# Expert rows added onto x by the gathering transfers, in the third attention

## The reference, cut to what matters

```
x = x + L1_ffn(layernorm(x))      # top 2 of 8 experts per token
x = x + L2_xattn(layernorm(x), ctx)

def L1_ffn(x):
    top_scores, token_idx, counts = route(x, gate_w, 8, 2)
    routed_in = x[token_idx] * top_scores[:, None]
    routed_out = grouped_swiglu(routed_in, w1, w2, w3, eid)
    return zeros.at[token_idx].add(routed_out)

def L2_xattn(x, context):         # 8 heads of 64, 64 keys per sequence
    q, k, v = x @ Wq, context @ Wk, context @ Wv
    return softmax(q k^T / 8) v @ Wo + bo
```

## Time and profile before

| | us |
|---|---|
| median of 3 runs (1964.0 to 1968.96) | 1968.83 |
| the profiled execution, its own time | 1969.98 |
| its span in the profile | 1967.4 |
| PE busy over the span | 1397.9 (71%) |
| DVE busy | 1165.4 (59%) |
| ACT busy | 714.6 (36%) |
| POOL busy | 590.0 (30%) |

### The profile page before, as it was taken

How to read it: one execution, slowest core, us unless ns; L and a number is a source line. 1 busy time by engine, 2 the same in 40 slices (tenths; PEclk the granted TensorE clock), 3 DMA queues, 4 the chain that set the end, 5 groups by cost and what they waited for, 6 DMA issues and landing times. The chain is left out here.

```text
span 1967.4 us, 43981 instructions
## 1 busy us (share of the span) xinstructions
PE 1397.9 (71%) x14780; PEld 1068.0 (54%) x14780; DVE 1165.4 (59%) x3326; ACT 714.6 (36%) x1769; POOL 590.0 (30%) x1118
## 2 busy tenths in 40 slices
PE   6999889965999730099948999740099646566564
PEld 3777645533777520099936888630088534454453
DVE  4888578877888760044424555460011179969896
ACT  2666456655666400022213455310033212232232
POOL 4555111112110116500047652117500187211231
PEclk9999956777999855599978999955599967677576
DMA  4222100000000001177731110001277511010001
GB/s 147 51 51 51 29 1 2 3 3 18 23 19 22 8 0 45 56 195 206 205 92 44 41 43 24 8 0 47 65 195 201 142 43 35 1 33 11 1 1 43
DMA packets 109071, 108.50 MB, mean 55 GB/s; under 512 B 12656, under 2 KB 88432, under 8 KB 108784
## 3 DMA queue, kind: packets, MB, share of 16 engines
q1 hardware_dynamic: 100720, 89.61, 16.7%
q0 software_dynamic: 8192, 16.79, 3.0%
HBM read 81.19 MB, written 25.17 MB: 54 GB/s over the span
## 5 line engine op out<-in xcount | busy, mean ns | idle before, releaser
L2223 DVE COPY e_xT<-e_pX 128x256 f32<-128x256 f32 x72 | 30.6, 425 | 317.2 <-PE e_pX L2284 317.2
L2284 PE MATMUL e_pX<-W,e_rows 128*128 128x128 f32 x144 | 28.7, 282 | 213.8 <-DMA e_rows<-slots_in 212.6
L2295 PE MATMUL e_H<-e_xT,e_w_up 128*128 128x256 f32 x736 | 174.9, 386 | 1.1 <-DMA e_w_up<-in_f_dram 1.1
L2295 PEld LDWEIGHTS e_H<-e_xT,e_w_up 128*128 128x128 f32 x736 | 136.9, 194 | 18.1 <-DVE e_xT L2223 1.5
L2284 PEld LDWEIGHTS e_pX<-W,e_rows 128*128 128x128 f32 x144 | 18.5, 147 | 216.4 <-DMA e_rows<-slots_in 216.0
L2305 PEld LDWEIGHTS e_pY<-e_w_down,e_h 128*128 128x128 f32 x992 | 119.6, 192 | 23.2 <-issue 16.6
L2305 PE MATMUL e_pY<-e_w_down,e_h 128*128 128x128 f32 x992 | 124.8, 277 | 10.2 <-ACT e_h L2272 9.0
L2144 POOL DMA_INDIRECT slots_in<-R,r_put x96 | 92.0, 959 | 57.1 <-issue 29.0
L428 DVE TENSOR_REDUCE a_mx<-a_S 128x8 f32<-128x1024 f32 x64 | 78.1, 1221 | 34.3 <-PE a_S L513 34.1
L473 ACT ACTIVATE a_PT<-a_ST 128x1024 f32<-128x1024 f32 x64 | 65.5, 1023 | 79.2 <-PE a_ST L540 79.2
L2261 ACT ACTIVATE e_silu<-e_H 128x256 f32<-128x256 f32 x120 | 46.0, 383 | 124.0 <-PE e_H L2295 124.0
(11 more groups left out here) (414 smaller groups left out, 4071.8 us busy)
## 6 DMA issues: line engine op xcount, KB each, us to landing
e_w_up<-in_f_dram SPq DMA_DIRECT2D x40, 384.0 KB, 3.7
e_w_down<-in_f_dram SPq DMA_DIRECT2D x32, 322.0 KB, 3.1
e_rows<-slots_in SPq DMA_DIRECT2D x72, 128.0 KB, 3.0
slots_out<-e_y SPq DMA_DIRECT2D x72, 128.0 KB, 3.6
e_w_up<-in_f_dram SPq DMA_DIRECT2D x32, 256.0 KB, 3.7
e_w_down<-in_f_dram SPq DMA_DIRECT2D x40, 192.0 KB, 3.3
slots_in<-Y SPq DMA_DIRECT2D x32, 160.0 KB, 2.5
a_cK<-in_ctxT_dram SPq DMA_DIRECT2D x64, 64.0 KB, 1.9
```

Source lines behind the costliest of these rows:

```text
L2295: i = nc.tensor.matmul(H[:, banks * p + b, CHUNK * c:CHUNK * (c + 1)], up[:, p, at:at + P], xT[:, p, :], start=True, stop=True)
```

## The change

POOL no longer adds rows. The two gathers of a tile write onto X itself, with an addition in the transfer; the second is issued only when the first has landed (`gather_onto_x`, k = 1). DVE waits for both of them itself (`rows_added`, in front of the statistics), and the statistics no longer wait for `s_x`. POOL's lags become 7 for the bias (8 before), 4 for `pool_rstd` (5 before), 0 for the first gather and 2 for the second. The order on POOL is bias, rstd, first gather, second gather. In this stage Y and R are no longer used. The whole diff:

```
--- before.py
+++ after.py
@@ -1108,7 +1108,7 @@
         s_pt, s_pts, s_o, s_rd, s_zn = [sem(n) for n in ("pt", "pt_out", "o", "rden", "zn")]
         s_zt, s_zts, s_y, s_x = [sem(n) for n in ("zt", "zt_out", "y", "x")]
         combine = Combine(net, net.routing, sem)
-        ln = LayerNorm(net, sb, sem, xn, s_xt, combine.s_x)
+        ln = LayerNorm(net, sb, sem, xn, s_xt, None)
         block = ctx.enter_context(nc.Block())
 
         @block.sync
@@ -1135,12 +1135,15 @@
                 done(pool, ln.s_xn, u)
                 nc.gpsimd.tensor_tensor(X[:, u, :], X[:, u, :], w("a2_bo"), ALU.add).then_inc(s_bo, 1)
 
-            pipeline(pool, NT, [(IN_FLIGHT + 4, add_bias), (IN_FLIGHT, lambda u, p: combine.add(pool, u)),
-                                (IN_FLIGHT + 1, lambda u, p: ln.pool_rstd(pool, u, p)),
-                                (0, lambda u, p: combine.gather(u))], straight=True)
+            pipeline(pool, NT, [(7, add_bias), (4, lambda u, p: ln.pool_rstd(pool, u, p)),
+                                (0, lambda u, p: combine.gather_onto_x(pool, u, 0)),
+                                (2, lambda u, p: combine.gather_onto_x(pool, u, 1))], straight=True)
 
         @block.vector
         def _(dve):
+            def rows_added(u, p):
+                combine.arrive(dve, u)
+
             def take_k(u, p):
                 done(dve, s_k, u)
                 free(dve, s_S, u)
@@ -1173,7 +1176,7 @@
                 nc.vector.tensor_tensor(X[:, u, :], pV[:, 0:128], X[:, u, :], ALU.add).then_inc(s_x, 1)
 
             pipeline(dve, NT, [(10, normalise), (7, softmax), (5, take_k),
-                               (0, lambda u, p: ln.vector_stats(dve, u, p)),
+                               (0, rows_added), (0, lambda u, p: ln.vector_stats(dve, u, p)),
                                (1, lambda u, p: ln.vector_moments(dve, u, p)),
                                (2, lambda u, p: ln.vector_apply(dve, u, p)), (11, residual)], straight=True)
 
@@ -2353,13 +2356,15 @@
         done(dve, self.s_first, u)
         v.tensor_tensor(pair(net.X, u), pair(net.X, u), rows[1], ALU.add).then_inc(self.s_x, 1)
 
-    def add(self, pool, u):
-        net = self.net
-        self.arrive(pool, u)
-        x, rows = net.X[:, u, :], (net.Y[:, u, :], net.R[:, u, :])
-        net.nc.gpsimd.tensor_tensor(x, x, rows[0], ALU.add).then_inc(self.s_first, 1)
-        done(pool, self.s_first, u)
-        net.nc.gpsimd.tensor_tensor(x, x, rows[1], ALU.add).then_inc(self.s_x, 1)
+    def gather_onto_x(self, pool, u, k):
+        rt, net = self.rt, self.net
+        got = rt.s_got[u % IN_FLIGHT]
+        rows = net.dram["slots_out"][0:NCH1 * CHUNK, :]
+        if k == 1:
+            pool.wait_ge(got, 16 * TOPK * (u // IN_FLIGHT) + 16)
+        net.nc.gpsimd.indirect_dma_start(
+            net.X[:, u, :], None, rows, bass.IndirectOffsetOnAxis(ap=rt.get[:, k, u:u + 1], axis=0),
+            compute_op=ALU.add).then_inc(got, 16)
 
 
 def mixture(net, first):
```

## The result

The changed kernel takes 1983.94 us (median of 4 runs, 1982.0 to 1987.88), the kernel before 1966.7 (4 runs). The ratio is 1.0081, 95% interval 1.0059 to 1.0103: slower by 12 to 20 us. The forecast was 1971.6 and no change within 0.3%; the range, 1962 to 1986, holds the time. Two rivals stood near this time, (c), the longer issue on POOL, at 1981.4, and (b), the slow landing, at 1983.4. The time alone doesn't tell them apart; the trace does, and it is (c).

The account below looks back on a forecast made before the run. POOL was taken to bound the fill, PE the rest. 2.6 us gained against 2.6 and 2.75 lost made 1969.98 into 1972.8, less 1.15 for the median: 1971.6; range 1962 to 1986, the forecast's own 1966 to 1977.

Parts of the forecast that it names:

- (c): POOL's issue grows by half, 0.48 us, for three row addresses per index; 12.6 us late at tile 11, 1981.4; chance 0.14.
- (b): Adding transfer lands like the slowest gather, 1.4 us later; period 6.79, tile 11 12.8 us late, 1983.4; chance 0.15.
- what bounds, and where: POOL sets the pipeline's fill, PE everything from 1100 on; the change's worth is read at tile 11's statistics.
- the loop and its sum: POOL's fill period per tile: rstd, two gather issues, landing, statistics; 5.39 us at plain gather prices, against 5.20 before.
- The gain without surcharge: At a plain gather's prices, tile 11's statistics in the fill start 2.6 us earlier: 1073.1 against 1075.68.
- the lever: Tile 11's delay in the fill from adding transfers' unknown issue and landing prices, called the whole case; 2.6 and 2.75 us.
- e: What adding adds to a transfer's landing after its issue; taken as 0.25 us, bounds -0.4 to 1.4.
- 26i + 11e: Shift of tile 11 in the fill from added issue and landing times, over nine periods and the start.
- i: What adding adds to a gather's issue on POOL; taken as 0.1 us, bounds 0 to 0.28.
- (a): Landing as quick as a scatter's, 2.2 us, issue free; tile 11 in the fill 7.0 us early, 1961.8; chance 0.16.
- (d): Both longer issue and slow landing; period 7.75, the loop bounds the whole stage, 46 us late, 2015; chance 0.07.
- PE's clock: Risk in the fill: idler PE runs one step's products at half speed, costing up to 5 us less the period's slack.

Follow-up runs that it names:

- e1: Changed kernel with both gathers plain, to Y and R, nothing added and expert rows left out; ratio 0.9984 to the kernel before.
- e2: Changed kernel with only the first gather of a tile adding, the second plain and its rows left out; ratio 1.0033 to the kernel before.
- e3: Changed kernel with only the second gather of a tile adding, the first plain and its rows left out; ratio 1.0023 to the kernel before.

## Why the prediction was right or wrong

**Right: what bounds, and where.** The fill is POOL's, the steady part PE's, and the loss that tile 11's statistics show (14.0 us) is the loss of the stage (14.7).

**Right: the loop and its sum.** 5.39 us with plain prices was 5.26 to 5.49 in eight of the nine periods from tile 2 to 11 of e1 and 6.21 in one. The gain without surcharge, 2.6 at tile 11, was 2.0; the one long period accounts for the difference.

**Right: the lever.** From a second gather's start to the statistics behind it the median of tiles 2 to 11 is 3.29 us in the changed kernel (3.23 to 3.39) and 2.60 in e1 (2.50 to 2.72, and 3.44 once); less the issue's 0.61 that leaves e = 0.08. 26i + 11e with i = 0.61 and this e gives 15.9 + 0.9 - 2.6 = 14.2; tile 11 lost 14.0. The halves of it, in e2 and e3, came within a microsecond.

**Wrong: the size of i.** "I take 0.1, nearer to 0, since there are as many indices as before" is the step that failed; it measured 0.61, and even the upper bound of 0.28 from rows of plain gathers was too low. A spread among operations of one kind does not bound another kind. It alone moves 0.51 x 26 = 13.3 us, and the forecast from no change to slower. The term e, taken at 0.25, was 0.08, and 1.9 us too dear. That the time still lies in the range is owed to the rivals that the range took in, and not to the forecast's own terms, which ended at 1977.

**Rival (c) was right in its time and not in its reason.** It priced i = 0.48 by three addresses per index for two. 0.48 is near, but with half the indices such a price would halve, and it fell from 0.61 to 0.53. The Trainium skill's rule ("Collectives: The Full Stack", The bandwidth ceiling), given there for the reduce step of a ring of cores, is that an addition in a transfer pays through a second read descriptor per chunk; it speaks of the transfer and not of POOL's issue, and is no measure of POOL's share here. The part that the transfer itself has, e, was 0.08 us. What these runs show of the transfers themselves is more and smaller packets: in the windows of the stage the software queue moved the same 4.20 MB in 9216 packets after and 2048 before.

**Rivals (a), (b) and (d)** fell: the landing beyond the issue grew by 0.08, neither shorter nor at 4.0. The period in the steady part, 6.73 on average (L231 at 1110.13 to 1204.35, 14 tiles), was just about PE's 6.70. (c) had 6.60 for the loop; with the measured terms its sum is 5.39 + 1.22 + 0.08 = 6.69, no longer hidden with room to spare. DVE did wait for rows in every tile (1.7 us each), which (b) had named as its sign, out of idle time that it had: the sign did not tell (b) from (c).

**PE's clock,** the side risk, was real and small: the granted clock was 0.94 for 1.00 in the third window. The products behind a stop show it: the scores at 1051.52 took 1.13 us, where the same 32 took 0.69 at 1058.25, and in e3 8 products took 1.97 us for 1.09.

## What to carry to other kernels

A transfer that adds saves an engine's addition and puts its own surcharge where it is issued: 0.61 us on POOL here, against the 0.46 us addition that it replaced. Before moving a wait closer to its transfer, write the loop down (issue, landing, consumer, next issue) and ask if the sum stays under the stage's period; one more step of lag turned this change from a loss into a gain. And an addition belongs in an idle gap of an engine's order, not just on an engine with idle time: the same two instructions end the stage 10 us later in one place than in another.

## What was not expected of the hardware

The issue of an indirect gather hardly depends on its size: 986 and 959 ns for 128 indices, 940 and 914 for 64. With an addition it is 1580, 1454 with 64 indices, and 1578 with 256-byte rows in place of 512. An addition on POOL right behind an adding gather is shown as starting 0.56 us before the gather's end (1060.56 against 1059.55 + 1.57) and ends only 0.50 after it, about the time that it takes alone.
